# Part of the edge records gathered inside layer 0's attention pass instead of ahead of it

## The chip, the cores and the metric

The kernel runs on one core of a Trainium2 chip. The metric is the device time of one execution in microseconds (us). The engines are named as in the profile: PE (TensorE), DVE (VectorE), ACT (ScalarE), POOL (GpSimd) and SP (SyncE). Each runs its own list of instructions, and they wait for each other through semaphores.

## What is computed

The reference is a graph network of four layers on 3125 nodes with 256 features and 100,000 edges. Each layer adds a graph part, a mixing part and a feed-forward part. The change concerns layer 0's graph part, and the edge records that layers 0, 2 and 3 share. Cut to that part:

```python
xn = _layernorm(x)
el = xn @ W_src + b_src
er = xn @ W_dst + b_dst
score = leaky_relu(el[src] + er[dst], 0.2) @ attn
ex = jnp.exp(score - segment_max(score, dst)[dst])
a = ex / segment_sum(ex, dst)[dst]
x = x + segment_sum(el[src] * a[:, None], dst) + mix(xn)
```

## The kernel before

**Nodes and edges.** The 3125 nodes are cut into 25 tiles of 125 (`TILES`, `R`). The edges are sorted by their target and cut into 784 chunks of 128 (`CHUNKS_S`); four chunks are a unit (`G`), which belongs to one tile of nodes. 196 units (`UNITS_1`) cover all chunks. 24 more units repeat the one unit that lies across each border of two tiles, which gives 220 (`UNITS_S`).

**Records.** For every edge a record of four numbers stands in memory: source node, edge weight, edge attribute and 1.0. After the sort, `o["row"]` holds the edge's number in the original order, and `fetch_records` (L545 on) gathers chunk after chunk of records into `o["record"]` with indirect DMAs on POOL. They go over eight lanes, each with its semaphore `fetched`; a gather waits until the one before it on its lane has landed. 280 chunks (`EARLY`, the sum of `SHARES`) are gathered during the phases ahead of layer 0. The other 504 are given to `open0` as its `pool_work`.

**Opening of layer 0** (`open0` in L1544, over `build_open`). It goes over the 25 tiles in five groups of five. DVE normalizes a group's rows; PE turns them (L1247) and multiplies them by the weights (L1486) in ten units per group of four matmuls each, into four PSUM buffers; ACT copies each unit out (`take_units`, L1454), and PE may not fill a PSUM buffer again before ACT has copied it. Then `post` works on the group on DVE, from L1571 to L1591, and PE adds up a product of keys and values (L1602). L1540 keeps that product at the end. Each group waits for a buffer of the group before, since there is only one `st`. POOL does nothing here but gather records.

**Unpacking** (`unpack_records`, L559 to L573). A phase of its own: DVE waits for all eight lanes, copies for each of the 24 repeated units the four chunks of records to the unit's own place (L571; the place comes out of a register loaded from `o["again"]`), and casts the source lane of all 880 chunks to integers, into `o["row"]` (L573).

**Attention pass** (`build_attend0`, L665). It goes through the 220 units in a pipeline of depth three. For unit u:

- POOL (`rows_of_unit`, L641 to L647, called at L697) gathers four chunks of `el` rows of 128 x 258 by `o["row"]`, into a ring of five slots (`LANES_A`). From the sixth unit on it waits for `summed` of the unit five before.
- DVE marks which node each edge belongs to (`mark_hots`, L657).
- PE turns the marks (L779); ACT copies them out twice (L838, L839).
- PE spreads the targets' rows over the edges (L789); DVE takes the maximum with the gathered rows (`lift`, L728) and reduces to scores (`measure`, L733, L735).
- PE spreads scores over nodes (L798); DVE raises the running maximum of each node (`raise_top`, L719 to L722).
- PE brings the maximum back to the edges (L805); DVE subtracts (`come_near`, L740, L741); ACT takes exponentials and scales the rows (`weigh`, L844 to L851; L848 copies the record's lanes 1 to 3 beside them).
- PE adds up rows by node (L813) and signals `summed`; DVE adds to the accumulator (`add`, L749, L750).

SP loads `attn` and writes zeros to `pairs` at the start. After the pass `bulk` copies the degrees (L2638). The same `rows_of_unit` and `o["row"]` serve layer 3's pass (lines L946 to L1173), and layers 1 and 2 have a simpler stage that sums gathered rows (`build_sums`, gathers L595, matmuls L631).

The order of the stages is that of the code: a phase ends on all engines before the next one begins.

## Time and profile before

| | |
|---|---|
| median of 3 executions | 11198.45 us (11197.33 to 11201.67) |
| profiled execution | 11192.64 us |
| its span | 11190.6 us |
| mean granted PE clock | 0.788 |
| opening, first to last group's L1571 | 1012.87 to 1625.49 us |
| attention pass of layer 0 | 1688 to 3145 us |

The span is the time from the first to the last instruction in the profile; the profiled execution took 2.04 us more. All positions below are in us from the span's start. The granted clock is given as a share of the full one. Line numbers (L647) are those of the kernel before. "Idle before" is the time that an engine stood still ahead of an instruction, with what ended it: an instruction of another engine, "issue" where the profile shows no wait, or "remote" where a semaphore came whose sender the profile doesn't name.

### The profile page before, as it was taken

The numbers are of one execution on the slowest core, as the hardware profiler recorded it, in microseconds if no ns is written. First come the engines' busy times: TensorE is split into PE (matmuls) and PEld (weight loads), VectorE is DVE, ScalarE is ACT, GpSimd is POOL, SyncE is SP. The second block draws the span as 40 slices with busy tenths as digits, with TensorE's granted clock in tenths as the row PEclk, the third lists the DMA queues.
The fourth block names the chain that finished last, engine by engine and source line by source line (L and its number), as shares of the span: only waits on it lengthen the run. The fifth ranks groups of instructions, "written<-read, shape, count | busy, mean of one in ns | idle before, by whom it ended". The sixth has DMA issues, their size and how long they took to land. (4 is left out here: it accounts for less than half of the span.)

```text
span 11190.6 us, 100099 instructions
## 1 busy us (share of the span) xinstructions
PE 6613.8 (59%) x28182; PEld 4970.1 (44%) x28182; DVE 4907.6 (44%) x13525; ACT 2129.1 (19%) x5700; POOL 4446.7 (40%) x4412
## 2 busy tenths in 40 slices
PE   0001228999966755556655555439566777774487
PEld 0000017888844433334433333328535666663355
DVE  7561137888844422223322222541225666665322
ACT  0000004444431200001200000122122333332222
POOL 0647735666600166662046665020205555550000
PEclk9997559999988877776767776659766777776699
DMA  0001003333300333331023332019502222220000
GB/s 12 6 13 16 4 8 105 82 83 83 83 15 8 108 93 93 93 93 40 10 69 94 92 94 77 0 24 312 193 19 71 71 71 72 71 69 6 10 11 17
DMA packets 404399, 696.90 MB, mean 62 GB/s; under 512 B 154143, under 2 KB 267784, under 8 KB 403421
## 3 DMA queue, kind: packets, MB, share of 16 engines
q0 software_dynamic: 206848, 480.68, 15.9%
q1 hardware_dynamic: 197076, 210.68, 5.9%
q8 instruction: 201, 3.29, 0.1%
q14 instruction: 274, 2.24, 0.1%
HBM read 631.46 MB, written 59.47 MB: 62 GB/s over the span
## 5 line engine op out<-in xcount | busy, mean ns | idle before, releaser
L647 POOL DMA_INDIRECT att_rows<-el_table,dst_order_row x1520 | 1560.2, 1026 | 1216.4 <-issue 369.5
L631 PE MATMUL sum_sum<-sum_rows,sum_hot 128*125 128x256 f32 x3520 | 1324.6, 541 | 1192.0 <-issue 477.9
L631 PEld LDWEIGHTS sum_sum<-sum_rows,sum_hot 128*125 128x125 f32 x3520 | 898.0, 268 | 1618.9 <-issue 526.3
L595 POOL DMA_INDIRECT sum_rows<-rel_table,src_order_row x880 | 843.6, 959 | 1162.1 <-ACTq L586 755.7
L595 POOL DMA_INDIRECT sum_rows<-el_table,dst_order_row x880 | 843.6, 959 | 967.0 <-ACTq L586 560.2
L550 POOL DMA_INDIRECT dst_order_record<-records,dst_order_row x784 | 813.6, 1038 | 588.1 <-PEq L454 297.1
L608 DVE TENSOR_TENSOR gnn_acc<-gnn_acc,sum_sum 125x256 f32 x440 | 184.4, 419 | 1869.3 <-DMA ffn0e_w<-in_L_ffn_eW_dram 603.0
L1111 PE MATMUL att_sum<-att_rows,att_hot 128*125 128x265 f32 x1280 | 456.4, 516 | 285.7 <-ACT att_rows L1173 169.9
L647 POOL DMA_INDIRECT dst_order_record<-el_table,dst_order_row x240 | 262.5, 1094 | 522.7 <-SPq L946 301.2
L1111 PEld LDWEIGHTS att_sum<-att_rows,att_hot 128*125 128x125 f32 x1280 | 301.4, 247 | 379.5 <-issue 302.8
L789 PE MATMUL att_found<-gnn_to_dst,att_hot_t 125*128 x1760 | 437.8, 392 | 3.9 <-ACT att_hot_t L838 3.1
L813 PE MATMUL att_sum<-att_rows,att_hot 128*125 128x261 f32 x1760 | 427.3, 385 | 2.4 <-ACT att_rows L851 2.4
L851 ACT ACTIVATE att_rows<-att_rows,att_p 128x257 f32<-128x257 f32 x880 | 375.7, 498 | 0.0
L1077 PEld LDWEIGHTS att_found<-layer_a_dst,att_hot_t 125*128 125x128 f32 x1760 | 314.7, 252 | 76.6 <-issue 45.9
L789 PEld LDWEIGHTS att_found<-gnn_to_dst,att_hot_t 125*128 125x128 f32 x1760 | 319.7, 192 | 39.4 <-issue 4.5
L813 PEld LDWEIGHTS att_sum<-att_rows,att_hot 128*125 128x125 f32 x1760 | 314.4, 189 | 47.9 <-ACT att_rows L851 2.5
L733 DVE CUSTOM_DVE_ANT_0 att_high<-att_high,att_att 128x256 f32<-128x256 f32 x880 | 319.9, 418 | 0.0
L1077 PE MATMUL att_found<-layer_a_dst,att_hot_t 125*128 x1760 | 278.5, 281 | 43.6 <-issue 28.4
L798 PE MATMUL att_spread_p<-ident,att_score 128*125 128x128 f32 x1760 | 251.3, 286 | 42.9 <-issue 26.7
L2739 POOL DMA_INDIRECT pairs<-XN,ffn_place x50 | 59.2, 1183 | 545.5 <-ACT XN L1425 527.4
L728 DVE TENSOR_TENSOR att_high<-att_rows,att_found 128x1024 f32<-128x1024 f32 x220 | 268.7, 1221 | 6.5 <-issue 6.5
L798 PEld LDWEIGHTS att_spread_p<-ident,att_score 128*125 128x125 f32 x1760 | 209.7, 188 | 130.4 <-issue 83.8
(776 smaller groups left out, 13008.8 us busy)
## 6 DMA issues: line engine op xcount, KB each, us to landing
block_w<-in_L_ffn_W_dram SPq DMA_DIRECT2D x112, 512.0 KB, 6.3
block_w<-in_L_ffn_W_dram SPq DMA_DIRECT2D x56, 1024.0 KB, 6.2
att_rows<-el_table,dst_order_row POOLq DMA_INDIRECT x1520
rel_table<-open_st SPq DMA_DIRECT2D x25, 784.0 KB
sum_rows<-rel_table,src_order_row POOLq DMA_INDIRECT x880
sum_rows<-el_table,dst_order_row POOLq DMA_INDIRECT x880
dst_order_record<-records,dst_order_row POOLq DMA_INDIRECT x784
pairs<-zeros SPq DMA_DIRECT2D x1, 7168.0 KB
```

What stands on the lines that cost most here:

```text
L550: nc.gpsimd.indirect_dma_start(o["record"][:, k, :], None, o["records"], bass.IndirectOffsetOnAxis(ap=o["row"][:, k:k + 1], axis=0)).then_ ...
L595: nc.gpsimd.indirect_dma_start(rows[l][:, g, :], None, table, bass.IndirectOffsetOnAxis(ap=o["row"][:, k:k + 1], axis=0)).then_inc(s[f"row ...
L631: last = nc.tensor.matmul(sums[u % SUMS][:, 0:D], hot[u % HOTS][:, g, :], rows[l][:, g, :], start=(g == 0), stop=(g == G - 1))
L647: nc.gpsimd.indirect_dma_start(rows[l][:, g, 0:width], None, table, bass.IndirectOffsetOnAxis(ap=o["row"][:, k:k + 1], axis=0)).then_inc(s ...
L728: v.tensor_tensor(high[:], rows[u % LANES_A][:, :, 0:D], found[:], ALU.max).then_inc(s["picked"], 1)
L733: last = v.tensor_tensor_reduce(high[:, g, :], high[:, g, :], att[:], 0.8, 0.0, ALU.mult, ALU.add, score[u % 2][:, g:g + 1])
L789: last = t.matmul(found[:, g, :], hot_t[u % TURNED][:, g * P:(g + 1) * P], nodes_of_unit(to_dst, tile), start=True, stop=True)
L798: last = t.matmul(spread_p[:, g * P:(g + 1) * P], score[u % 2][:, g:g + 1].to_broadcast([P, R]), c["ident"][:], start=True, stop=True)
L813: last = t.matmul(sums[u % 2][:, 0:S], hot[u % HOTS][:, g, :], rows[u % LANES_A][:, g, :], start=(g == 0), stop=(g == G - 1))
L851: last = a.activation(own_rows[:, g, 0:D + 1], own_rows[:, g, 0:D + 1], ACT.Copy, scale=p[u % 2][:, g:g + 1])
L1077: done = t.matmul(found[u % 2][:, g, 0:H], hot_t[u % 2][:, g * P:(g + 1) * P], nodes_of_unit(to_dst, tile), start=True, stop=True)
L1111: done = t.matmul(sums[u % 2][:, 0:W + 1], hot[u % HOTS_B][:, g, :], rows[u % LANES_B][:, g, :], start=(g == 0), stop=(g == G - 1))
```

## The change

`open0` is given only the record gathers 280 to 549 (`OPENING = EARLY + 270`). The other 234 are issued by POOL in the attention pass: behind the four row gathers of unit u, records up to number 550 + (u + 1) * 5 // 4, so one, one, one and two in each four units, until all 784 are under way behind unit 187.

The phase `unpack_records` is gone. The source lane is stored as integer bits in the record, and the row gathers of layer 0 take their index straight from it. POOL waits for the four chunks' `fetched` ahead of each of the first 196 units, and for a new semaphore `repeated` ahead of each of the last 24. The copies of the 24 repeated units are made by DVE in the pass (`repeat`), at the head of its loop turns 188 to 211: a register load and two copies each, one for the integer lane and one for the other three. `o["row"]`, which layer 3 reads, is filled by one copy in the phase that copies the degrees, after the pass.

```diff
--- before.py
+++ after.py
@@ -38,6 +38,7 @@
 REC_LANES = 8
 SHARES = (14, 190, 30, 6, 8, 18, 14)
 EARLY = sum(SHARES)
+OPENING = EARLY + 270
 
 
 
@@ -152,7 +153,7 @@
                 v = nc.vector
                 v.memset(rec[:, :, 3], 1.0).then_inc(s["packed"], 1)
                 dve.wait_ge(s["loaded"], 48)
-                v.tensor_copy(rec[:, :, 0], src_i[:]).then_inc(s["packed"], 1)
+                v.tensor_copy(rec[:].bitcast(I32)[:, :, 0], src_i[:]).then_inc(s["packed"], 1)
                 v.tensor_copy(rec[:, :, 1], parts["weight"][:]).then_inc(s["packed"], 1)
                 v.tensor_copy(rec[:, :, 2], parts["attr"][:]).then_inc(s["packed"], 1)
 
@@ -556,23 +557,6 @@
     return lambda pool: fetch_records(nc, pool, o, sum(SHARES[:n]), sum(SHARES[:n + 1]))
 
 
-def unpack_records(nc, c, o):
-
-    with phase(nc, "unpack", "chain") as s, nc.Block() as block:
-        @block.vector
-        def _(dve):
-            v = nc.vector
-            own = Chain(dve, s["chain"])
-            for lane in range(REC_LANES):
-                dve.wait_ge(o["fetched"][lane], 16 * (CHUNKS_S // REC_LANES))
-            for b in range(TILES - 1):
-                at = dve.value_load(o["again"][0:1, b:b + 1], min_val=0, max_val=CHUNKS_S - G)
-                to = CHUNKS_S + b * G
-                last = v.tensor_copy(o["record"][:, to:to + G, :], o["record"][:, bass.ds(at, G), :])
-            own(last)
-            own(v.tensor_copy(o["row"][:], o["record"][:, :, 0]))
-
-
 def build_sums(nc, c, tag, table, o, w, acc):
 
 
@@ -681,10 +665,11 @@
         score, near, p = [[sb(f"{n}{l}", [P, G]) for l in range(2)] for n in ("score", "near", "p")]
         new, fall, corr = [[sb(f"{n}{l}", [R, 1]) for l in range(2)] for n in ("new", "fall", "corr")]
         top, best = sb("top", [R, TILES, 1]), sb("best", [R, 1])
+        src = o["record"][:].bitcast(I32)
         turn_p, found, spread_p, place_p = ps("turn_p", [R, G * P]), ps("found", [P, G, D]), ps("spread_p", [R, G * P]), ps("place_p", [P, 512])
         sums = [ps(f"sum{l}", [R, 512]) for l in range(2)]
         names = ["loaded", "cleared", "hot_ready", "turned", "hot_t_ready", "mask_ready", "found", "picked", "scored", "spread", "topped", "placed", "near_ready",
-                 "corr_ready", "p_ready", "scaled", "summed", "added", "chain"] + [f"rows_in{l}" for l in range(LANES_A)]
+                 "corr_ready", "p_ready", "scaled", "summed", "added", "repeated", "chain"] + [f"rows_in{l}" for l in range(LANES_A)]
         with phase(nc, "att0", *names) as s, nc.Block() as block:
             @block.sync
             def _(sp):
@@ -694,7 +679,22 @@
 
             @block.gpsimd
             def _(pool):
-                rows_of_unit(nc, pool, s, table, o, rows, W, LANES_A)
+                fetched = OPENING
+                for u in range(N):
+                    l = u % LANES_A
+                    if u >= LANES_A:
+                        pool.wait_ge(s["summed"], u - LANES_A + 1)
+                    if u < UNITS_1:
+                        for k in range(u * G, u * G + G):
+                            pool.wait_ge(o["fetched"][k % REC_LANES], 16 * (k // REC_LANES + 1))
+                    else:
+                        pool.wait_ge(s["repeated"], u - UNITS_1 + 1)
+                    for g in range(G):
+                        nc.gpsimd.indirect_dma_start(rows[l][:, g, 0:W], None, table, bass.IndirectOffsetOnAxis(ap=src[:, u * G + g, 0:1], axis=0)
+                                                     ).then_inc(s[f"rows_in{l}"], 16)
+                    more = min(CHUNKS_S, OPENING + (u + 1) * 5 // 4)
+                    fetch_records(nc, pool, o, fetched, more)
+                    fetched = more
 
             @block.vector
             def _(dve):
@@ -749,8 +749,20 @@
                     v.scalar_tensor_tensor(to[:, 0:D + 1], to[:, 0:D + 1], corr[u % 2][:], sums[u % 2][:, 0:D + 1], ALU.mult, ALU.add)
                     v.tensor_tensor(to[:, D + 1:], to[:, D + 1:], sums[u % 2][:, W:S], ALU.add).then_inc(s["added"], 1)
 
+                def repeat(b):
+
+                    if b == 0:
+                        for lane in range(REC_LANES):
+                            dve.wait_ge(o["fetched"][lane], 16 * (CHUNKS_S // REC_LANES))
+                    at = dve.value_load(o["again"][0:1, b:b + 1], min_val=0, max_val=CHUNKS_S - G)
+                    to = slice(CHUNKS_S + b * G, CHUNKS_S + b * G + G)
+                    v.tensor_copy(src[:, to, 0], src[:, bass.ds(at, G), 0])
+                    v.tensor_copy(o["record"][:, to, 1:], o["record"][:, bass.ds(at, G), 1:]).then_inc(s["repeated"], 1)
+
                 make_hot(0)
                 for u in range(N + 2):
+                    if 0 <= u - UNITS_1 + 8 < TILES - 1:
+                        repeat(u - UNITS_1 + 8)
                     if u + 1 < N:
                         make_hot(u + 1)
                     if 1 <= u <= N:
@@ -2628,14 +2640,14 @@
 
     with nc.sbuf_tensor("gnn0_to_dst", [R, TILES, D], F32) as to_dst:
         m["to_dst"] = to_dst
-        open0(nc, c, m, I, dram, lambda pool: fetch_records(nc, pool, by_dst, EARLY, CHUNKS_S))
-        unpack_records(nc, c, by_dst)
+        open0(nc, c, m, I, dram, lambda pool: fetch_records(nc, pool, by_dst, EARLY, OPENING))
         with nc.sbuf_tensor("gnn0_acc", [R, TILES, D + 4], F32) as acc:
             build_attend0(nc, c, by_dst, dram["el0"], to_dst, I["L0_gnn_attn"], acc, dram["pairs"])
 
             def keep(v, own, act_step):
 
                 own(v.tensor_copy(m["deg3"][:], acc[:, :, D + 1:].rearrange("p t k -> p k t")))
+                own(v.tensor_copy(by_dst["row"][:], by_dst["record"][:].bitcast(I32)[:, :, 0]))
             bulk(nc, "degrees", keep)
             close0(nc, c, m, I, acc)
     experts0(nc, c, m, I)
```

## Rows read from the trace of the kernel before

**Rows 1.** The page: busy us of each engine (share of the span), instructions.

```profile
PE 6613.8 (59%) x28182; PEld 4970.1 (44%) x28182; DVE 4907.6 (44%) x13525; ACT 2129.1 (19%) x5700; POOL 4446.7 (40%) x4412
```

**Rows 2.** Timeline of DVE in the opening: start, us, instruction [idle before <-releaser].

```profile
1216.67 1.51 DVE L1571 TENSOR_TENSOR open_row<-open_st,open_bias 125x1280 f32<-125x1280 f32 x1 [138.70 <-issue]
...
1423.94 1.49 DVE L1571 TENSOR_TENSOR open_row<-open_st,open_bias 125x1280 f32<-125x1280 f32 x1 [138.68 <-issue]
...
1569.41 1.49 DVE L1571 TENSOR_TENSOR open_row<-open_st,open_bias 125x1280 f32<-125x1280 f32 x1 [76.91 <-ACT open_st L1454]
...
1625.49 1.49 DVE L1571 TENSOR_TENSOR open_row<-open_st,open_bias 125x1280 f32<-125x1280 f32 x1 [22.51 <-ACT open_st L1454]
```

**Rows 3.** Timeline of ACT, and of POOL's last record gather, in the opening.

```profile
1204.66 0.59 ACT L1454 COPY open_st<-open_unit 125x512 f32<-125x512 f32 x1 [10.62 <-remote]
...
1536.42 0.94 POOL L550 DMA_INDIRECT dst_order_record<-records,dst_order_row  x1 [0.30 <-issue]
...
1562.37 2.22 ACT L1454 COPY open_st<-open_unit 125x512 f32<-125x512 f32 x4 [2.23 <-remote]
```

**Rows 4.** Stretches: us, then PE, PEld, DVE, ACT, POOL busy (count), clock, DMA, GB/s.

```profile
1217.00:1424.00 207.00, 37.29 (x70) 16.65 (x70) 37.01 (x36) 10.04 (x15) 160.98 (x152) 0.56 0.06 5
1900.00:2900.00 1000.00, 961.89 (x5563) 804.98 (x5562) 821.21 (x3093) 482.68 (x1392) 616.58 (x619) 1.00 0.31 83
1945.60:1950.60 5.00, 4.76 (x30) 3.91 (x30) 4.03 (x19) 2.43 (x8) 4.00 (x4) 1.00 0.29 78
3871.00:5121.00 1250.00, 660.42 (x1750) 449.14 (x1751) 318.56 (x1099) 0.00 (x0) 843.00 (x880) 0.73 0.32 92
8378.40:8392.70 14.30, 10.14 (x40) 8.87 (x40) 3.71 (x12) 2.19 (x7) 10.86 (x12) 0.52 0.36 96
```

**Rows 5.** Timeline of POOL and ACT at the start of layer 3's pass.

```profile
8378.49 0.97 POOL L647 DMA_INDIRECT dst_order_record<-el_table,dst_order_row  x1 [301.24 <-SPq L946]
...
8400.32 0.59 ACT L1137 COPY att_hot_t<-att_turn_p 125x512 f32<-125x512 f32 x1 [11.17 <-DMA combine_rows<-results,ffn_place]
...
8430.43 0.59 ACT L1137 COPY att_hot_t<-att_turn_p 125x512 f32<-125x512 f32 x1 [29.43 <-issue]
```

**Rows 6.** Timeline of POOL, PE and DVE at the start of layer 0's pass.

```profile
1688.97 0.95 POOL L647 DMA_INDIRECT att_rows<-el_table,dst_order_row  x1 [151.60 <-POOLq L84]
...
1705.21 1.04 PE L798 MATMUL att_spread_p<-ident,att_score 128*125 128x128 f32 x8
...
1711.42 0.69 DVE L719 CUSTOM_DVE_ANT_0 att_mask<-att_mask,att_spread_p 125x512 f32<-125x512 f32 x1 [6.03 <-remote]
```

**Rows 7.** Timeline of POOL in layer 0's pass: first gathers of two units.

```profile
1945.65 0.94 POOL L647 DMA_INDIRECT att_rows<-el_table,dst_order_row  x1 [1.55 <-PE att_sum L813]
...
1952.12 0.94 POOL L647 DMA_INDIRECT att_rows<-el_table,dst_order_row  x1 [1.56 <-PE att_sum L813]
```

**Rows 8.** Groups of instructions, 1900 to 2900 us: busy, mean ns, idle before.

```profile
L647 POOL DMA_INDIRECT att_rows<-el_table,dst_order_row x619 | 617.4, 997 | 384.7 <-PE att_sum L813 242.1 <-issue 142.6
...
L740 DVE TENSOR_TENSOR att_near<-att_score,att_place_p 128x4 f32<-128x4 f32 x155 | 24.5, 158 | 118.2 <-PE att_place_p L805 107.6 <-issue 10.6
```

**Rows 9.** Groups of instructions on POOL from 334 to 1211 us.

```profile
L550 POOL DMA_INDIRECT dst_order_record<-records,dst_order_row x549 | 559.2, 1019 | 516.4 <-PEq L454 297.1 <-issue 163.9 <-PEq L1985 18.7
```

**Rows 10.** Timeline of DVE between the opening and the pass.

```profile
1666.14 0.62 DVE L1540 SCALAR_TENSOR_TENSOR KV<-open_kv_p,block 128x128 f32<-128x128 f32 x2 [7.06 <-PEq L84]
...
1669.18 0.17 DVE L571 COPY dst_order_record<-dst_order_record 128x16 f32 x1 [2.43 <-issue]
...
1686.49 0.94 DVE L573 CAST dst_order_row<-dst_order_record 128x880 int32<-128x880 f32 x1
...
1688.39 0.08 DVE L704 MEMSET att_top<- 125x25 f32 x1 [0.96 <-PEq L84]
```

**Rows 11.** Timeline of POOL in the first part of layer 1's sums.

```profile
3914.22 0.95 POOL L595 DMA_INDIRECT sum_rows<-rel_table,src_order_row  x1 [1.68 <-DMA ffn0e_w<-in_L_ffn_eW_dram]
...
3922.65 0.95 POOL L595 DMA_INDIRECT sum_rows<-rel_table,src_order_row  x1 [3.72 <-DMA ffn0e_w<-in_L_ffn_eW_dram]
```

## The prediction

> **What bounds the kernel now.** The page comes first: the span is 11190.6 us and no engine fills it (PE, the busiest, 59%) [rows 1], so stages are read one by one. The change touches two: the opening of layer 0 with the unpacking behind it, and layer 0's attention pass. The clock in the pass is full (1.00) [rows 4].
>
> Opening: the timeline of DVE shows when each of the five groups gets its first step, L1571. Two groups apart while record gathers run: 1423.94 - 1216.67 = 207.3 us. Behind the last gather (1536.42): 1625.49 - 1569.41 = 56.1 us [rows 2, 3]. It is the same work. The timeline of ACT shows why: its copies L1454 each idle 10.62 us before they run for 0.59, released by "remote", in a stretch where PE is busy 37 of 207 us [rows 3, 4]. Within 26 us of POOL's last gather the wait is down to 2.23 us for four copies together. A copy takes over a unit of four matmuls and four weight loads; (10.62 + 0.59) / 8 = 1.40 us per PE instruction. So I read: while POOL issues indirect gathers with no pause, what PE has finished is told to the others at one instruction per 1.40 us.
>
> The start of layer 3's pass shows that this begins late. Gathers run in a row from 8378.49; PE executes 40 matmuls and 40 loads by 8392.70, and the copy that waits for the last of them starts at 8400.32, 7.7 us late. By then (21.8 us) 15.6 instructions were told at 1.40 us each, so about 80 - 16 = 64 fit into a store ahead of the delay. Then it is slow: the next copy idles 29.43 us [rows 4, 5]. At the start of layer 0's pass (gathers in a row from 1688.97) it is less: L798's result, done at 1706.25 as 64th PE instruction, frees L719 at 1711.42, 22.5 us after the first gather: 64 - 16 = 48 [rows 6]. The store holds 48 to 64.
>
> The pass: 619 row gathers in 1000 us are 154.75 units, 6.46 us each [rows 4, 8]. PE is busy 96% and DVE 82%. POOL issues four gathers in 4.91 us (a lone one takes 0.94 behind a gap of 0.30 [rows 3], so about 1.25 each), then rests 1.56 us until `summed` frees a ring slot [rows 7]. In a burst of 5.0 us PE issues 60 instructions [rows 4]; less 3.6 told, 56 are pending: within the store, and the pause clears it. PE issues 72 a unit (5563 + 5562 over 154.75).
>
> **The change, part by part**, against the profiled execution (11192.64 us: span 11190.6 and 2.04 around it; 5.8 under the median 11198.45).
>
> 1. Opening. 280 records come before this stage; 270 more is number 550, which is issued at about 1211 (549 gathers began by then) [rows 9]. Instead of going on to 1536, POOL stops there. Group 2's step at 1216.67 comes as before; the third follows after 56.1 + 3 for the store to clear (it took 25 us behind the last gather before, mostly beside work), the next two after 56.1: 1217 + 59 + 56 + 56 = 1388 against 1625.49. I take **-235** (bounds -225 and -245: 10 us either way for the clearing). The rest of the stage is equal. The gathers themselves were not the path: the delay they cause was.
>
> 2. Unpacking. 24 copies L571 and the cast L573 run from 1669.18 to 1687.43, behind a change of phase: the last KV step ends at 1666.76 and the pass's first memset is at 1688.39 [rows 10]. Without them 1688.39 - 1666.76 = 21.6, less 2.43 for the one change of phase left: **-19**.
>
> 3. They come back in the pass as `repeat`: a register load and two copies. One copy with its load took (1686.49 - 1669.18) / 24 = 0.72 us; a second copy adds about 0.15. DVE idles per unit 118.2 / 155 = 0.76 us before L740 [rows 8, 10], and the copies stand ahead of the work that PE waits for; I take no cover: 24 x 0.85 = **+20** (bounds +2, all in that idle time, and +20). The first repeat waits for all lanes, long landed: POOL is units ahead.
>
> 4. The cast moved behind the pass: 0.94 us as before, **+1**. The integer record in place of the float: same copies, 0. POOL's waits on `fetched` (four a unit) find records landed at least 32 gathers ahead: 0, unless each costs issue time; bounded above by one more gap of 0.30 us a unit, which goes into rival (a).
>
> Fixed part: -235 - 19 + 20 + 1 = **-233**.
>
> 5. The pass. 234 gathers are spread over 188 units, 1.25 each. None of their data is late; they lengthen POOL's burst. 4.91 + 1.25 x 1.25 = 6.47 us a unit, as long as the unit itself (6.46), and with the gap before the next gather 6.77: POOL has no pause left. In such a burst PE issues 72 and 4.6 are told: 67 pending, above the store of 48 to 64. So the hand-overs stop before the burst ends. Who is late: ACT's L838 and DVE's L719 and L740 behind PE, then PE behind them, then `summed`, for which POOL waits once its five slots are full. POOL is therefore given a pause, but only by the engines having stood still: a unit takes the burst plus a pause in which the store clears and `summed` comes. The pause's length: now 1.56 us, with the store not full [rows 7]; in the sums' stage, with long bursts, 1.68 and 3.72 us [rows 11]. I take 2.0, near the lower, since here the store overflows by a few instructions and not by dozens: 6.47 + 2.0 = 8.5 us a unit. (8.5 - 6.46) x 188 = **+383**. Bounds: 1.56 gives 8.03 and +295; 3.72 gives 10.2 and +700. A pause of 3.0, (9.5 - 6.46) x 188 = +565, is where I end the range, since only one of two rows lies beyond.
>
> Sum: -233 + 383 = +150: 11192.6 + 150 = 11343, and 5.8 more on the median's level: **11348**.
>
> The Trainium skill speaks against part 5: in "SBUF — State Buffer", "SBUF: two separate sides", it says "A DMA cannot be slowed by a compute op, and vice versa", and lays what looks like it to descriptor writing alone. By that rule more gathers beside PE and DVE would delay no hand-over and the sum would be rival (a)'s. The waits of 10.62 us [rows 3] and 29.43 us [rows 5] don't fit it.
>
> **Rivals.** (a) *POOL alone is the bound, hand-overs undisturbed.* For it: the pass today runs in step, though 56 instructions are pending at a burst's end; the store may be larger than I read. Against it: with no pause at all the backlog never clears, whatever the store. A unit would take 6.77 us, (6.77 - 6.46) x 188 = +58, or with the 0.30 of part 4 7.07 and +115: -175 to -118, so 11023 to 11080 on the median's level. It ends on the other side. It decides if a unit takes under 6.46 + 233 / 188 = 7.70 us. Chance 0.20.
>
> (b) *As in the sums' stage*, where POOL issues 880 gathers in 1250 us, 1.42 us each with its pauses [rows 4, 11]: 5.25 x 1.42 = 7.46 us a unit, +188, so -45 and 11153. For it: it is the one long stage of bursts that the trace has. Against: PE issues 3500 instructions in those 1250 us, 2.8 per us against 11, so its store fills four times slower. Chance 0.15; a third of it falls within the band around no change (7.59 to 7.82 us a unit).
>
> (c) *The moved gathers do nothing in the opening*, because the opening's groups are late for another reason: then only -19 + 20 + 1 and the pass's cost are left, +385 and more, 11580. Against it: the last group runs in 56.1 us the moment that POOL has stopped [rows 2]. Chance 0.05 with all beyond my range.
>
> (d) *The pass's cost meets the gain by chance*: 0.03.
>
> My forecast (units of 7.9 to 9.5 us): 0.57.
>
> **How the numbers follow.** The time is the likeliest case's: 11348; its own range is 11260 (pause 1.56) to 11530 (pause 3.0). The full range reaches down into rival (a), to 11040, with less than half of it left out (0.08), and up to 11560, with (c) left out (0.05) and a little of mine. What a measurement of this kernel can tell from no change is 0.2%, 22 us. Faster: (a) 0.20 and two thirds of (b) 0.10: 0.30. Same: a third of (b) and (d): 0.08. Slower: 0.57 + 0.05: 0.62.
>
> **What would show each step.** Opening: L1571's last at about 1388, and the steps 56 us apart after 1217; if they stay 200 apart, (c). L571 gone; the pass begins about 254 us earlier, near 1434. Pass: 5.25 gathers a unit; a unit's length by L728's count in 1000 us: 118 for me, 148 for (a), 134 for (b). ACT's L838 and DVE's L719 or L740 with idle times of 1 to 3 us put down to "remote" or "issue", PE's busy share down from 96% to some 73%, and POOL's rest 2 us a unit; under (a) POOL shows no rest but 0.30 us gaps and the hand-overs no delay. After unit 188 the last 32 units, without record gathers, should be back at 6.46 us, 7.3 with a repeat. Later stages: equal to 2 us. What would make me wrong above all: a store deeper than 67, or one that clears in gaps as short as 0.30 us beside a mixed load; and, on the other side, a lower granted clock once PE idles a quarter of the time (0.73 in the sums' stage), which would come on top.

## The result, and the profile after

The changed kernel took 11295.19 us (median of 4, 11284.83 to 11308.2); the kernel before took 11199.35 (median of 4) beside it. The ratio is 1.0086, with an interval of 1.0071 to 1.0101: slower by 96 us. The profiled execution has a span of 11289.6 us, 99.0 more than before. The experiments below ran on several chips, and on one of them the same change made the kernel faster by 2%; what the trace of this section shows is a chip on which it is slower.

**Opening.** Timeline of DVE, the answer to [rows 2] and [rows 10]: the five groups' first steps (now L1583), the last step of the stage, and the attention pass's first instruction.

```profile
1019.92 1.55 DVE L1583 TENSOR_TENSOR open_row<-open_st,open_bias 125x1280 f32<-125x1280 f32 x1 [97.20 <-issue]
...
1224.43 1.49 DVE L1583 TENSOR_TENSOR open_row<-open_st,open_bias 125x1280 f32<-125x1280 f32 x1 [137.20 <-ACT open_st L1466]
...
1285.63 1.49 DVE L1583 TENSOR_TENSOR open_row<-open_st,open_bias 125x1280 f32<-125x1280 f32 x1 [21.12 <-ACT open_st L1466]
...
1346.95 1.49 DVE L1583 TENSOR_TENSOR open_row<-open_st,open_bias 125x1280 f32<-125x1280 f32 x1 [21.13 <-ACT open_st L1466]
...
1403.22 1.49 DVE L1583 TENSOR_TENSOR open_row<-open_st,open_bias 125x1280 f32<-125x1280 f32 x1 [22.68 <-ACT open_st L1466]
...
1443.96 0.62 DVE L1552 SCALAR_TENSOR_TENSOR KV<-open_kv_p,block 128x128 f32<-128x128 f32 x2 [7.16 <-PEq L85]
...
1445.55 0.08 DVE L704 MEMSET att_top<- 125x25 f32 x1 [0.97 <-ACTq L85]
```

The second step stands where it stood; behind it the groups are 61.2, 61.3 and 56.3 us apart instead of 207, 145 and 56. The stage from its first L1583 to the KV step takes 424.0 us where it took 653.3 [rows 10; the first step was then at 1012.87]: -229.2. The whole stage begins 7.1 us later in this trace; in the seven other traces from such chips it began between 1013 and 1036, so this is scatter of the stages ahead and not the change's. The pass begins 1.6 us behind the KV step where it began 22.3 behind: the unpacking's -20.7.

Timeline of ACT in the same place, against [rows 3]: the last copies under record gathers wait as before. POOL's last gather is at 1212.19, and the copy that comes 10.5 us behind its end still waits 9.22 us. In the next groups the copies that follow each other wait 0.8 to 1.1 us, for PE.

```profile
1202.61 0.58 ACT L1466 COPY open_st<-open_unit 125x512 f32<-125x512 f32 x1 [10.62 <-remote]
...
1223.62 0.58 ACT L1466 COPY open_st<-open_unit 125x512 f32<-125x512 f32 x1 [9.22 <-remote]
```

**Pass.** The stretch from 1900 to 2900 us in the view of stretches (length, then PE, PEld, DVE, ACT and POOL busy, clock, DMA), against the second of [rows 4]:

```profile
1900.00:2900.00 1000.00, 820.53 (x4367) 690.91 (x4366) 646.41 (x2427) 382.15 (x1092) 627.47 (x638) 0.92 0.25 65
```

PE executes 4367 matmuls where it executed 5563; a unit has 36, so these are 121.3 units, 8.24 us each instead of 6.46. The granted clock of the stretch is 0.92 where it was 1.00, and a matmul takes 188 ns of PE's busy time on the mean where it took 173. That makes 0.54 us a unit; how much of it is part of the 1.78 us that a unit has become longer, no run separates. The groups of POOL's and then of ACT's instructions in that stretch, against [rows 8] (`L693` gathers rows, `L551` records):

```profile
L693 POOL DMA_INDIRECT att_rows<-el_table,dst_order_record x486 | 484.1, 996 | 326.8 <-PE att_sum L825 150.3 <-issue 120.9 <-DMA el_table<-open_row 34.9
L551 POOL DMA_INDIRECT dst_order_record<-records,dst_order_row x152 | 143.9, 947 | 46.3 <-issue 46.3
```

```profile
L850 ACT COPY att_hot_t<-att_turn_p 125x512 f32<-125x512 f32 x121 | 70.8, 585 | 334.0 <-PE att_turn_p L791 184.1 <-remote 148.4 <-issue 1.6
```

And of DVE's:

```profile
L719 DVE CUSTOM_DVE_ANT_0 att_mask<-att_mask,att_spread_p 125x512 f32<-125x512 f32 x121 | 83.1, 687 | 172.1 <-remote 122.3 <-PE att_spread_p L810 39.3 <-issue 8.3
...
L740 DVE TENSOR_TENSOR att_near<-att_score,att_place_p 128x4 f32<-128x4 f32 x122 | 19.3, 158 | 141.9 <-remote 94.3 <-PE att_place_p L817 47.5
```

Of ACT's 334 us of idle time before its copy L850, 148 are released by "remote"; in the case followed below, the sender was long done by then. Two thirds of DVE's waits before L719 and L740 are of that kind too. Before the change L740 waited almost only for PE, 0.76 us a unit [rows 8]. The timelines of POOL, and of ACT with the PE instructions that its first copy waits for, show in two neighbouring units how it looks:

```profile
2041.41 0.94 POOL L551 DMA_INDIRECT dst_order_record<-records,dst_order_row  x1 [0.30 <-issue]
...
2044.67 0.94 POOL L693 DMA_INDIRECT att_rows<-el_table,dst_order_record  x1 [2.32 <-PE att_sum L825]
...
2049.87 0.94 POOL L551 DMA_INDIRECT dst_order_record<-records,dst_order_row  x1 [0.30 <-issue]
...
2054.08 0.94 POOL L693 DMA_INDIRECT att_rows<-el_table,dst_order_record  x1 [3.26 <-PE att_sum L825]
```

```profile
2040.28 1.22 PE L791 MATMUL att_turn_p<-ident,att_hot 128*125 128x128 f32 x4
...
2044.35 0.58 ACT L850 COPY att_hot_t<-att_turn_p 125x512 f32<-125x512 f32 x1 [4.90 <-remote]
...
2052.08 0.58 ACT L850 COPY att_hot_t<-att_turn_p 125x512 f32<-125x512 f32 x1 [2.93 <-PE att_turn_p L791]
```

PE ended the turn that ACT's copy waits for at 2041.50; the copy starts at 2044.35, 2.9 us late, when POOL has stopped for 2.0 us. POOL's rest ends when L825 has handed over, 2.32 and 3.26 us after its last gather.

**The repeats and the end.** Timeline of DVE: two of the 24 repeats, and the copies behind the pass.

```profile
3015.14 0.17 DVE L759 COPY dst_order_record<-dst_order_record 128x4 int32 x1 [0.71 <-issue]
...
3022.29 0.24 DVE L759 COPY dst_order_record<-dst_order_record 128x4 int32 x1 [0.32 <-issue]
...
3247.24 0.28 DVE L2649 COPY deg<-gnn_acc 125x75 f32<-125x75 f32 x1 [0.90 <-PEq L85]
...
3247.55 0.94 DVE L2650 COPY dst_order_row<-dst_order_record 128x880 int32<-128x880 int32 x1
```

Units with a repeat follow each other every 7.11 us. From the first memset to the degrees' copy the pass takes 1801.7 us; before it took 1456.7 (1688.39 to 3145.09): +345.0. All together: +7.1 - 229.2 - 20.7 + 345.0 - 3.1 (all later stages) = +99.1.

### The profile page after: what moved, and what is told of

It is laid out like the page before. It is cut to its first block and busy times, and to the rows that moved or that the text cites. A ratio compares the mean times of both kernels' runs of the same rounds, so it can differ in the third digit from the quotient of the medians.

```text
span 11289.6 us, 100538 instructions
## 1 busy us (share of the span) xinstructions
PE 6693.5 (59%) x28182; PEld 5053.6 (45%) x28182; DVE 4912.7 (44%) x13549; ACT 2132.8 (19%) x5700; POOL 4413.4 (39%) x4412
## 5 line engine op out<-in xcount | busy, mean ns | idle before, releaser
L693 POOL DMA_INDIRECT att_rows<-el_table,dst_order_record x880 | 880.6, 1001 | 833.0 <-PE att_sum L825 299.0
L551 POOL DMA_INDIRECT dst_order_record<-records,dst_order_row x784 | 780.3, 995 | 588.2 <-PEq L455 297.0
L631 POOL DMA_INDIRECT att_rows<-el_table,dst_order_row x640 | 683.5, 1068 | 510.5 <-PE att_sum L1123 345.3
L801 PE MATMUL att_found<-gnn_to_dst,att_hot_t 125*128 x1760 | 482.1, 421 | 17.6 <-DVE att_high L728 12.9
L825 PE MATMUL att_sum<-att_rows,att_hot 128*125 128x261 f32 x1760 | 432.3, 388 | 2.4 <-ACT att_rows L863 2.4
L801 PEld LDWEIGHTS att_found<-gnn_to_dst,att_hot_t 125*128 125x128 f32 x1760 | 344.9, 206 | 65.7 <-issue 21.6
L810 PE MATMUL att_spread_p<-ident,att_score 128*125 128x128 f32 x1760 | 281.7, 310 | 154.4 <-issue 120.4
L810 PEld LDWEIGHTS att_spread_p<-ident,att_score 128*125 128x125 f32 x1760 | 249.3, 215 | 228.8 <-issue 156.0
L825 PEld LDWEIGHTS att_sum<-att_rows,att_hot 128*125 128x125 f32 x1760 | 320.5, 192 | 48.9 <-ACT att_rows L863 2.5
L817 PEld LDWEIGHTS att_place_p<-att_new,att_hot_t 125*128 125x128 f32 x1760 | 240.0, 202 | 151.5 <-DVE att_top L722 135.6
```

Of the source, the lines that this page charges most:

```text
L551: nc.gpsimd.indirect_dma_start(o["record"][:, k, :], None, o["records"], bass.IndirectOffsetOnAxis(ap=o["row"][:, k:k + 1], axis=0)).then_ ...
L631: nc.gpsimd.indirect_dma_start(rows[l][:, g, 0:width], None, table, bass.IndirectOffsetOnAxis(ap=o["row"][:, k:k + 1], axis=0)).then_inc(s ...
L693: nc.gpsimd.indirect_dma_start(rows[l][:, g, 0:W], None, table, bass.IndirectOffsetOnAxis(ap=src[:, u * G + g, 0:1], axis=0)).then_inc(s[f ...
L801: last = t.matmul(found[:, g, :], hot_t[u % TURNED][:, g * P:(g + 1) * P], nodes_of_unit(to_dst, tile), start=True, stop=True)
L810: last = t.matmul(spread_p[:, g * P:(g + 1) * P], score[u % 2][:, g:g + 1].to_broadcast([P, R]), c["ident"][:], start=True, stop=True)
L825: last = t.matmul(sums[u % 2][:, 0:S], hot[u % HOTS][:, g, :], rows[u % LANES_A][:, g, :], start=(g == 0), stop=(g == G - 1))
```

## The experiments

The twelve runs fell on six chips of two kinds, and each kernel is compared with the kernel before on its own chip. Chips are called *late* and *prompt* here. On chips of the late kind the kernel before takes 11198 to 11224 us and its hand-overs wait as in [rows 3]; the traces ahead of this section are of that kind. On chips of the prompt kind it takes 10629 to 10633 us. The first four runs were on a prompt chip, which I hadn't known of when I wrote their expectations.

**All records in the opening** (prompt chip, then again on a late one). Nothing is moved, but the unpacking stays gone.

```diff
-OPENING = EARLY + 270
+OPENING = CHUNKS_S
```

> All 504 record gathers go back into the opening; the pass has only its four row gathers a unit, but the unpacking stays gone and its copies stay in the pass. My theory (the moved gathers alone cost and gain): the opening as before (last L1571 near 1625), the pass at 6.46 us a unit, the 24 repeats 0.62 us each as measured in the changed kernel (+15), one copy +1, the unpacking's -21: about -5 us against the kernel before, 0.9995 of it. Rival (the new way of indexing and of waiting costs in each unit): the pass longer by 220 times 0.1 to 1 us, so +20 to +200.

Measured: 0.9993 (0.9984 to 1.0003), 10628 us. The size is as forecast, but the opening isn't. Timeline of DVE in the opening (first two groups, then the KV step), and one of POOL's gathers long behind them:

```profile
853.99 1.49 DVE L1583 TENSOR_TENSOR open_row<-open_st,open_bias 125x1280 f32<-125x1280 f32 x1 [21.57 <-ACT open_st L1466]
...
915.44 1.49 DVE L1583 TENSOR_TENSOR open_row<-open_st,open_bias 125x1280 f32<-125x1280 f32 x1 [21.05 <-ACT open_st L1466]
...
1472.59 0.62 DVE L1552 SCALAR_TENSOR_TENSOR KV<-open_kv_p,block 128x128 f32<-128x128 f32 x2 [344.02 <-PEq L85]
```

```profile
1149.67 0.94 POOL L551 DMA_INDIRECT dst_order_record<-records,dst_order_row  x1 [0.30 <-issue]
```

The groups follow each other every 61.5 us under uninterrupted gathers of 1.25 us each. No copy of ACT waits for "remote". All five groups are done near 1129, and the engines then wait 344 us for POOL. There the gathers themselves set the opening's length, and not what they do to others.

**One record gather in two units** (prompt).

```diff
-OPENING = EARLY + 270
+OPENING = EARLY + 410
-more = min(CHUNKS_S, OPENING + (u + 1) * 5 // 4)
+more = min(CHUNKS_S, OPENING + (u + 1) // 2)
```

> Only 94 record gathers are moved, one in every second unit of the first 188; the other 410 stay in the opening. Opening: POOL stops near 1395 instead of 1212, so the last L1571 should come near 1515, -110 against before. Pass, my theory (a rest of POOL clears the store): every second unit keeps its rest of 1.56 us, so the hand-overs hold and the pass costs 0 to 30 us: -130 to -95 in all. Rival one (a constant price for each moved gather, 1.41 us as in the changed kernel): +133, so about 0 in all. Rival two (POOL alone is the bound): cost 0, as my theory; the two are not told apart here but in the next.

Measured: 0.9886 (0.9870 to 0.9903), 10515 us. The stretch of the pass from 1400 to 2400 us:

```profile
1400.00:2400.00 1000.00, 961.73 (x5562) 804.73 (x5561) 822.08 (x3092) 482.32 (x1391) 689.22 (x696) 1.00 0.32 83
```

696 gathers in 1000 us, and still 154.5 units: the added ones cost nothing here. The gain is the 94 gathers' time in the opening.

**One in each unit** (prompt): `OPENING = EARLY + 316`, `more = min(CHUNKS_S, OPENING + u + 1)`.

> 188 record gathers are moved, one in each of the first 188 units: POOL's work is 5 gathers, 4.91 + 1.25 + 0.30 = 6.46 us a unit, as long as the unit. Opening about -215 against before. My theory: no rest is left, the store runs over in nearly each unit, 7.9 us a unit: +270, so +40 to +60 in all. Rival (POOL alone is the bound): 6.5 us a unit, +8, so -220 in all.

Measured: 0.9780 (0.9763 to 0.9796), 10405 us. My theory is wrong on this chip, and the rival right. The same stretch, and ACT's copy in it:

```profile
1400.00:2400.00 1000.00, 956.70 (x5535) 801.33 (x5534) 824.22 (x3072) 479.43 (x1383) 765.72 (x770) 1.00 0.32 83
```

```profile
L850 ACT COPY att_hot_t<-att_turn_p 125x512 f32<-125x512 f32 x154 | 90.1, 585 | 247.9 <-PE att_turn_p L791 247.9
```

770 gathers, POOL all but without a rest (its idle time elsewhere is the 0.30 us gap), 153.8 units, and no "remote".

**Iotas in place of the moved gathers** (prompt, then late). All records are gathered in the opening; in the pass POOL computes 234 iotas whose numbers nobody uses.

```diff
-                    fetch_records(nc, pool, o, fetched, more)
+                    for n in range(min(234, u * 5 // 4), min(234, (u + 1) * 5 // 4)):
+                        if n >= 2:
+                            pool.wait_ge(s["filled"], n - 1)
+                        nc.gpsimd.iota(filler[n % 2][:], [[1, 990]], base=0,
+                            channel_multiplier=990).then_inc(s["filled"], 1)
```

> All record gathers in the opening, and in the pass POOL computes an iota of 128 x 990 integers (about 0.95 us) wherever the changed kernel gathers records. The iotas' numbers are not used. My theory (what hinders the hand-overs is the issuing of indirect gathers, and an iota is a rest from it): no 'remote' waits, 6.5 to 6.8 us a unit, +10 to +60 against the kernel with all in the opening. Rival (how long POOL is busy decides): 8.2 us a unit as in the changed kernel, +330.

Measured on the prompt chip: 1.0005 (0.9996 to 1.0015). It tells nothing there, since no hand-over is late in any run.

> The kernel with 234 iotas in the pass in place of record gathers, once more: its fourth run fell on a chip where no hand-over is late. If this chip is of the other kind (kernel before near 11199): my theory (indirect gathers in a row hold the hand-overs, an iota is a rest from them) gives 6.5 to 6.9 us a unit and +10 to +80 against before; the rival (a busy POOL holds them, whatever it does) 8.2 us a unit and +320, as with the spare gathers. If it is of the first kind (before near 10633): +4 us as there.

Measured on a late chip: 0.9986 (0.9976 to 0.9995), 11188 us. The stretch, POOL's groups and ACT's copy:

```profile
1900.00:2900.00 1000.00, 957.88 (x5540) 801.62 (x5539) 820.29 (x3076) 480.19 (x1385) 832.88 (x808) 1.00 0.31 83
```

```profile
L694 POOL DMA_INDIRECT att_rows<-el_table,dst_order_record x617 | 650.8, 1055 | 166.4 <-issue 165.7 <-PE att_sum L827 0.7
L699 POOL IOTA att_filler<- 128x990 int32 x191 | 183.3, 973 | 1.0
```

```profile
L852 ACT COPY att_hot_t<-att_turn_p 125x512 f32<-125x512 f32 x153 | 89.7, 586 | 241.8 <-PE att_turn_p L793 135.3 <-issue 106.5
```

POOL is busy 833 of 1000 us, more than in the changed kernel (627), yet 153.9 units pass, 6.50 us each, and no wait is "remote"; ACT's copy idles 242 us in all, as in the kernel before (239). A busy POOL is not what holds the hand-overs; its indirect gathers are. Whether it is their issuing or their transfers, the iotas, which have neither, don't tell.

**Spare gathers** (late). All records in the opening, and in the pass 234 of them gathered a second time, into a place that nobody reads.

```diff
+                    for n in range(min(234, u * 5 // 4), min(234, (u + 1) * 5 // 4)):
+                        lane, turn = n % REC_LANES, n // REC_LANES
+                        if turn:
+                            pool.wait_ge(s[f"extra_in{lane}"], 16 * turn)
+                        nc.gpsimd.indirect_dma_start(extra[lane][:], None, o["records"], ...
```

> All record gathers in the opening, as in the kernel of the first run, and in the pass POOL gathers 234 records a second time into a spare place, at the changed kernel's places (POOL does this work in addition, its result is not used). It is the pass of the changed kernel with the opening of before. If hand-overs are on time on this chip: 6.5 to 6.8 us a unit over 188 units, +10 to +57 against the kernel before, less 5. If they are late as in the changed kernel's trace (8.2 us a unit): +330. With the iotas' +4 us of the fourth run it says what a gather costs more than an iota.

Measured: 1.0291 (1.0274 to 1.0308), 11522 us, +323. ACT's copy in the pass:

```profile
L857 ACT COPY att_hot_t<-att_turn_p 125x512 f32<-125x512 f32 x123 | 72.1, 586 | 343.1 <-PE att_turn_p L798 175.8 <-remote 160.5 <-issue 6.8
```

The index in the record, the waits on `fetched` and the repeats stay in this kernel, and so they do in the one with all records in the opening, whose pass takes 1469.2 us on a late chip (the last run below). The spare gathers are what differs, and with them the pass takes 1795.0. So the cost is that of the gathers themselves; no record that the pass needs is moved into it.

**The changed kernel beside others** (late, late, prompt).

> The changed kernel itself, beside the kernel before on the same chip. In the first four runs no hand-over was late and the kernel before took 10633 us instead of 11199. If this chip is of that kind: the opening is bound by POOL's gathers, 234 fewer of them end it 234 x 1.25 = 293 us earlier but not before the engines' own end near 1150, so about 288; POOL alone bounds the pass at 6.5 to 6.8 us a unit, +10 to +57; unpacking and repeats -5: -280 to -235 against before, 0.974 to 0.978 of it. If the chip is of the kind of the first two traces (hand-overs late while gathers run, before near 11199): +97 as measured there. Rival to the chip as the cause (the change is slower everywhere): slower here too by 0.9%.

Measured, late: 1.0091 (1.0074 to 1.0108).

> The changed kernel on this call's chip. If the kernel before is near 10633 here: -280 to -235, for the opening is bound by POOL's gathers there and the pass stays near 6.5 to 6.8 us a unit. If it is near 11199: +97 to +102, as twice before.

Measured, late again: 1.0086 (1.0069 to 1.0103).

> The changed kernel beside the kernel before, in the hope of a chip that hands over on time (before near 10633), on which it hasn't run yet. There the kernel with one record gather a unit took 228 us less than before: its pass began 231 us earlier. The changed kernel moves 46 gathers more, 46 x 1.25 = 57 us earlier still, and its pass is bound by POOL at 5.25 gathers, 6.77 us a unit at most, 188 x 0.25 = 47 us over that kernel's: -240, between -280 and -225. On a chip that hands over late: +97 to +102 as three times before.

Measured, prompt: 0.9800 (0.9784 to 0.9817), 10413 us, -217, a little outside what I gave. The stretch, POOL's groups and ACT's copy:

```profile
1400.00:2400.00 1000.00, 910.36 (x5192) 779.21 (x5191) 771.28 (x2888) 450.81 (x1299) 769.43 (x757) 0.98 0.30 78
```

```profile
L693 POOL DMA_INDIRECT att_rows<-el_table,dst_order_record x577 | 590.8, 1024 | 175.8 <-issue 170.3 <-PE att_sum L825 5.5
L551 POOL DMA_INDIRECT dst_order_record<-records,dst_order_row x180 | 179.9, 999 | 54.8 <-issue 54.8
```

```profile
L850 ACT COPY att_hot_t<-att_turn_p 125x512 f32<-125x512 f32 x144 | 84.3, 585 | 247.0 <-PE att_turn_p L791 247.0
```

POOL has no rest; 144.2 units of 6.93 us. Four gathers under DVE's work and 1.25 more with their gaps are what a unit takes, so this is rival (a) to the letter: it gave 6.77 to 7.07. The kernel with one gather a unit has the lower ratio of the two, 0.978 against 0.980, but their intervals overlap.

**The two other densities on a late chip.**

> 94 record gathers in the pass, one in every second unit, once more. If this chip holds hand-overs late (kernel before near 11199): opening about -110; pass by my theory (a rest of 1.56 us in every second unit clears the store) 0 to +30, so -125 to -95 in all with the unpacking and the repeats; by the rival (a constant price of 1.41 us for each moved gather, as in the changed kernel) +133, about 0 in all. If hand-overs are on time here (before near 10633): -1.1% as in the second run.

Measured: 1.0065 (1.0048 to 1.0082), 11267 us. I had expected the store to clear in every second unit. The stretch and ACT's copy:

```profile
1900.00:2900.00 1000.00, 897.25 (x5044) 757.86 (x5043) 747.35 (x2801) 437.44 (x1260) 623.38 (x631) 0.97 0.28 75
```

```profile
L850 ACT COPY att_hot_t<-att_turn_p 125x512 f32<-125x512 f32 x140 | 81.9, 585 | 353.6 <-PE att_turn_p L791 177.0 <-remote 144.9 <-issue 31.7
```

140.1 units, 7.14 us each. The timeline of POOL shows two neighbouring units (first and last gather of each, and the next first):

```profile
2101.66 0.94 POOL L693 DMA_INDIRECT att_rows<-el_table,dst_order_record  x1 [4.10 <-PE att_sum L825]
...
2106.87 0.94 POOL L551 DMA_INDIRECT dst_order_record<-records,dst_order_row  x1 [0.30 <-issue]
...
2109.06 0.94 POOL L693 DMA_INDIRECT att_rows<-el_table,dst_order_record  x1 [1.25 <-DMA dst_order_record<-records,dst_order_row]
...
2113.16 0.95 POOL L693 DMA_INDIRECT att_rows<-el_table,dst_order_record  x1 [0.30 <-issue]
...
2115.08 0.94 POOL L693 DMA_INDIRECT att_rows<-el_table,dst_order_record  x1 [0.97 <-PE att_sum L825]
...
2120.07 0.94 POOL L551 DMA_INDIRECT dst_order_record<-records,dst_order_row  x1 [0.30 <-issue]
```

The unit with five gathers is followed by an idle 1.25 us, the one with four by 0.97, and ahead of 2101.66 stand 4.10 behind late hand-overs: the rest comes in lumps of many sizes, and no unit clears the store for the next. (The profile puts the 1.25 down to the landing of a record, but the records that this unit needs had been issued some 400 gathers earlier.) On the mean of the stretch the rest is (1000 - 623.4 - 631 x 0.30) / 140.1 + 0.30 = 1.64 us a unit, nearly what it was before the change (1.58 by the same sum from [rows 4]).

> 188 record gathers in the pass, one in each unit, once more. If this chip holds hand-overs late: opening -190 to -215; pass by my theory (burst of 6.16 us, rest under 0.3, store full) near 7.9 us a unit, +270, so +30 to +70 in all; by the rival (a threshold above five gathers a unit) 6.5 us a unit, +10, so -200 in all. If hand-overs are on time here: -2.2% as in the third run.

Measured: 1.0062 (1.0045 to 1.0079), 11270 us; the stretch, 126.1 units of 7.93 us:

```profile
1900.00:2900.00 1000.00, 845.37 (x4541) 706.32 (x4540) 674.06 (x2532) 399.08 (x1140) 628.16 (x633) 0.94 0.26 68
```

**All records in the opening, on a late chip.**

> All record gathers in the opening, unpacking gone, once more. If this chip holds hand-overs late: -21 (unpacking) +15 (repeats) +1: -5, at most -20 where the scatter ahead of the opening helps, 0.998 to 1.000, so the best of the versions there, ahead of the changed kernel by 100 us. The rival, that its repeats and index loads cost more under late hand-overs: above 1.000. If hand-overs are on time here: 0.999 as in the first run.

Measured: 0.9993 (0.9984 to 1.0002), 11221 us. The timeline of DVE, first group and KV step:

```profile
1036.01 1.49 DVE L1583 TENSOR_TENSOR open_row<-open_st,open_bias 125x1280 f32<-125x1280 f32 x1 [110.68 <-issue]
...
1671.53 0.62 DVE L1552 SCALAR_TENSOR_TENSOR KV<-open_kv_p,block 128x128 f32<-128x128 f32 x2 [5.74 <-PEq L85]
```

635.5 us for the opening, where the changed kernel takes 424.0 and the kernel before 653.3. With all gathers in it the opening took 648.6 and 649.9 in two other traces, so it scatters by some 18 us. The pass takes 1469.2 us, 12.5 more than before, which I put down to the 24 repeats.

**The passes side by side**, from the first memset to the degrees' copy. "Extra" is against the kernel with all records in the opening on a chip of the same kind (1469.2 us late, 1461.7 prompt), divided by the number of moved, spare or replaced gathers:

| in the pass | late: extra, per one | prompt: extra, per one |
|---|---|---|
| 94 gathers | 134.6, 1.43 | 1.4, 0.01 |
| 188 gathers | 267.7, 1.42 | 7.8, 0.04 |
| 234 gathers (the change) | 332.5, 1.42 | 76.9, 0.33 |
| 234 spare gathers | 325.8, 1.39 | not run |
| 234 iotas | 1.2, 0.01 | 16.2, 0.07 |

Each entry is one trace. The changed kernel's two other traces on late chips give 333.1 and 342.7. The execution behind the entry of 94 gathers on a late chip was 23 us shorter than its kernel's median; if that lay in the pass, the price would be 1.68.

## Why the prediction was right

It gave 11348 us, a range of 11040 to 11560 and slower at 0.62; 11295 was measured. By its steps:

1. *Opening, -235 (-225 to -245).* Measured -229.2. I took 56 us for each group behind POOL's end. That is the last group's time; those that have another group to prepare take 61.3, on both kinds of chip. The group that I let begin 59 us behind the second began 61.2 behind it, and the steps behind that one came as far apart, so no 3 us for the store to clear are seen.
2. *Unpacking, -19.* Measured -20.7. *Repeats, +20.* Measured +12.5, 0.52 each: less than the 0.85 of the copies, so a part seems to be hidden in DVE's idle time, of which I had counted none. *The moved cast, +1.* L2650 takes 0.94.
3. *The waits on `fetched`, 0.* POOL's gaps between gathers stay at 0.30.
4. *The pass, +383 (8.5 us a unit).* Measured +332.5, 8.24 us a unit. The burst of 6.47 us holds: 5.25 gathers at the measured spacings. The mis-sized term is the pause: I took 2.0 us, it is (1000 - 627.5 - 638 x 0.30) / 121.3 + 0.30 = 1.79. The lower clock that I had named as coming on top is in it (0.92). It also shows in PE's busy share, which fell to 82% and not to 73%: fewer matmuls, each of them longer. (For the range's end, 9.5 - 6.46 should have been 9.47 - 6.46, which is what +565 comes from.)
5. *The store of 48 to 64 instructions as the reason that four gathers are harmless and 5.25 are not.* This fell, though it gave the right sign. By it, one gather in two units costs next to nothing; it costs 1.43 us, as any other. The pause of 2.0 us was chosen with this store as its reason, so that it came near 1.79 is luck. What the runs show in its place is a steady account: under late hand-overs a unit takes its gathers' time and a rest of 1.6 to 1.8 us on top (1.64 with 4.5 gathers, 1.74 with 5, 1.79 with 5.25, all worked out as above). So an added gather costs its whole 1.25 us and the growth of the rest. With four gathers the same sum gives 1.58, but that says nothing of late hand-overs: a unit takes 6.47 us on a prompt chip too (first run, 1500 to 2500 us: 5564 matmuls), and POOL rests 1.60 there. That the two lengths meet just at four gathers is my reading of the three denser kernels; no kernel with fewer than four was run. The store shows at a row's start alone [rows 5, 6].
6. *Rival (a), POOL alone is the bound, 0.20.* It is refuted for the late chips by the 148 us of "remote" waits and by the iotas, which keep POOL busier and cost 1.2 us in all. On the prompt chips it is what happens. It is the most that I missed: I weighed (a) as another reading of one machine, and it was the right reading of another one. That the forecast was right in sign hung on the chip: mine was written from the trace of a late chip and met a late chip, and nothing in it foresaw the other kind. *(b), 7.46 us a unit:* no run with 5.25 gathers came near it. *(c):* refuted by the groups 61 us apart.

The sum on a late chip: a gather costs 0.98 us in the opening (229.2 / 234) and 1.42 in the pass, so moving it loses. With 94 and 188 gathers moved the opening took 566.7 and 452.9 us, which is 0.92 and 1.07 for each against the 653.3 of before; the scatter of 18 us named above is in these figures. On a prompt chip it costs 1.23 to 1.26 (the KV step came 117.3, 231.4 and 295.6 us earlier for 94, 188 and 234 gathers) and 0.01 to 0.33, so moving it gains, up to the five gathers that fill a unit.

The Trainium skill's rule that a DMA and a compute operation don't slow each other ("SBUF — State Buffer", "SBUF: two separate sides") agrees with the prompt chips, where 770 gathers in 1000 us left no "remote" wait and units of 6.50 us. On the late chips the stage is slowed by gathers that nothing else in it waits for, which the rule doesn't foresee; but the rule is about the ports of SBUF, and no run here shows that these are where the delay arises.

No version beats the kernel before on both kinds: one gather in each unit is best on prompt chips (0.978) and loses 0.6% on late ones; with all records in the opening the kernel is level on both.

Open stays what makes a chip late. The runs name the condition (POOL's indirect gathers, and not its other work), and a price for each stage: 11.2 us from copy to copy in the opening, 1.42 us for an added gather in the pass. The prediction's 1.40 us for each PE instruction carries over to no pass: a unit has 72 of them and takes 8.24 us. Nor is a rest a cure at once: behind POOL's last gather in the opening 10.5 us went by until ACT's next copy, while in the pass rests of 1.8 us are enough to keep going. The runs don't show the path on which a semaphore waits, nor why two chips of six never showed it. With gathers issued from another engine's queue it wasn't tried.

## What to carry to other kernels

Look for waits that end on "remote" or "issue" long after their sender was done, and see which engine issues DMAs through them: a queue of transfers that looks like free background work can set the pace of engines that it shares no data with. Price such a transfer in every stage where it could go, by the length of that stage with and without it, and not by its own 1.25 us: here the same gather cost 0.98 in one stage and 1.42 in the other. And when a change's sign hangs on a behaviour of that kind, time it on more than one chip before it is kept or dropped.

## What was not expected of the hardware

- Two kinds of chip: the kernel before takes 10629 to 10633 us on two of them and 11198 to 11224 on four, 5.4% apart. An opening group under gathers takes 61.5 us on the first kind and 204 to 207 on the second. In the pass with four gathers a unit the granted clock was 1.00 on either.
- The late hand-over is tied to indirect gathers and not to POOL's being busy: 833 us of work in 1000 with iotas in it leaves hand-overs on time, 627 us of gathers alone doesn't.
- On late chips the number of gathers that the pass issues in 1000 us hardly moves with their density: 619, 631, 633 and 638. On prompt ones it rises from 619 (none moved) to 770 (one in each unit). The changed kernel, with 5.25 a unit, has 757 there.
